# Quantised blocks: the second half of each normalisation moves from ScalarE to VectorE and GpSimd

## What is computed

```python
h = x
for blk in range(3):
    i0, i1 = (2 * blk, 2 * blk + 1)
    y = _qlora_linear(h, qweights[i0], scales[i0], biases[i0], lora_a[i0], lora_b[i0])
    y = _layernorm(y, ln_gamma[blk], ln_beta[blk])      # (y - mu) * rsqrt(var + 1e-5) * g + b
    y = jax.nn.gelu(y, approximate=False)
    y = _qlora_linear(y, qweights[i1], scales[i1], biases[i1], lora_a[i1], lora_b[i1])
    h = y + h
return h
```

## Time and profile before

| | |
|---|---|
| median of 3 runs | 1666.32 us |
| lowest and highest of them | 1662.14 and 1670.17 us |
| the profiled execution, own time | 1663.76 us |
| its span, first to last instruction | 1661.5 us |
| mean granted TensorE clock | 0.964 of full speed |
| busy share of the span: PE, DVE, ACT, POOL | 88%, 65%, 55%, 40% |

### The profile page before, as it was taken

The page is one execution under the profiler, slowest core; times in us unless marked ns, Lnnn a source line. Parts: engine busy times, 40 slices in busy tenths (PEclk is TensorE's granted clock), DMA queues, the critical chain, the costliest instruction groups (busy, mean ns, idle before and its releaser), DMA issues. The chain is left out here.

```text
span 1661.5 us, 30953 instructions
## 1 busy us (share of the span) xinstructions
PE 1470.2 (88%) x10541; PEld 1027.0 (62%) x10541; DVE 1079.1 (65%) x2724; ACT 920.5 (55%) x2444; POOL 658.3 (40%) x863
## 2 busy tenths in 40 slices
PE   7999999889989998999999895889889686999976
PEld 5667666666666665778787663555557533555643
DVE  5588888875666654555444346777523387899964
ACT  3578888555555563544544341334444258878945
POOL 5799999611111001003220253314534303888820
PEclk8999999999999997999999997999999887999999
DMA  9000000000000003000000114000012212333300
GB/s 296 14 1 14 14 15 15 13 1 1 1 1 1 1 1 119 1 2 21 18 17 21 44 60 173 2 1 13 30 54 61 75 35 47 90 85 87 91 12 25
DMA packets 48433, 65.36 MB, mean 39 GB/s; under 512 B 7839, under 2 KB 34568, under 8 KB 47530
## 3 DMA queue, kind: packets, MB, share of 16 engines
q1 hardware_dynamic: 43738, 54.02, 11.0%
q0 software_dynamic: 4544, 9.38, 1.6%
HBM read 52.80 MB, written 15.77 MB: 41 GB/s over the span
## 5 line engine op out<-in xcount | busy, mean ns | idle before, releaser
L2412 POOL TENSOR_TENSOR weighted<-state,c_all 128x512 f32<-128x512 f32 x128 | 163.5, 1297 | 78.7 <-DVE state L2422 64.8
L798 ACT ACTIVATE probs<-psum_all,pair_shift 128x256 f32<-128x256 f32 x256 | 117.8, 472 | 77.2 <-POOL pair_shift L487 77.2
L2422 DVE TENSOR_TENSOR_SCAN state<-decay,psum_all 128x512 f32<-128x512 f32 x128 | 149.0, 1200 | 14.3 <-PE psum_all L2340 11.5
L971 DVE TENSOR_REDUCE pair_negmax<-psum_all 128x2 f32<-128x512 f32 (+1 forms) x192 | 114.9, 639 | 55.9 <-PE psum_all L657 55.3
L2049 POOL DMA_INDIRECT found<-values,dest x78 | 74.7, 957 | 156.1 <-ACT values L2042 138.8
L798 ACT ACTIVATE probs<-psum_all,pair_negmax 128x192 f32<-128x192 f32 (+1 forms) x192 | 81.5, 436 | 93.6 <-DVE pair_negmax L971 46.3
L500 POOL TENSOR_SCALAR probs<-probs,pair_recip 128x256 f32<-128x256 f32 x128 | 121.8, 959 | 5.1 <-DVE pair_recip L991 5.1
L809 ACT ACTIVATE probsT<-psum_all 128x512 f32<-128x512 f32 x224 | 122.5, 612 | 0.3 <-PE psum_all L672 0.3
L2350 PE MATMUL psum_all<-weighted,ident 128*128 128x512 f32 x256 | 121.7, 600 | 0.0
L672 PE MATMUL psum_all<-ident,probs 128*128 128x128 f32 x896 | 116.7, 273 | 0.1
L487 POOL TENSOR_SCALAR pair_shift<-pair_negmax,row_term 128x1 f32<-128x1 f32 x256 | 102.2, 418 | 34.9 <-DVE pair_negmax L971 34.9
(11 more groups left out here) (402 smaller groups left out, 3510.5 us busy)
## 6 DMA issues: line engine op xcount, KB each, us to landing
c_all<-c_rows SPq DMA_DIRECT2D x64, 256.0 KB, 3.3
slots<-slot_fill_dram SPq DMA_DIRECT2D x2, 2535.0 KB, 14.4
ring<-slots SPq DMA_DIRECT2D x18, 260.0 KB, 2.9
keys<-found SPq DMA_DIRECT2D x16, 256.0 KB, 4.6
scale_rows<-row_scales SPq DMA_DIRECT2D x8, 256.0 KB, 4.6
up<-up_dram SPq DMA_DIRECT2D x1, 2048.0 KB, 7.8
down<-down_dram SPq DMA_DIRECT2D x1, 2048.0 KB, 13.0
up<-up_dram SPq DMA_DIRECT2D x1, 1408.0 KB, 6.1
```

The source lines that it names most:

```text
L798: nc.scalar.activation(k.probs[:, 2 * (u % PAIR_BUF) + j, t, key_cols(u, t)], k.psum[score_bank(u, j)][:, score_cols(u, t)], ACT.Exp, bias ...
L971: nc.vector.reduce_max(k.pair_negmax[:, u % 2, SUB * j:SUB * (j + 1)], src, AXX, negate=True).then_inc(s.negmax_ready, 1)
L2412: nc.gpsimd.tensor_tensor(w.weighted[:, u % RING, :], w.state[:, u % RING, :], w.c_all[:, u // L3_DC % C_RING, :], ALU.mult)\
L2422: nc.vector.tensor_tensor_scan(w.state[:, u % RING, :], w.decay[:, u % L3_RING, :, :].rearrange("p b n -> p (b n)"), k.psum[u % PARTS_RING ...
```

## The change

VectorE and GpSimd normalise the tiles of a block's second couple (chunks 2 and 3): GpSimd the first tile of each chunk (`BY_POOL` = 1), VectorE the other three. Each subtracts the mean and multiplies by rstd in one `tensor_scalar`, so the second couple needs no `scales`. ScalarE does root and both normalises for the first couple, then only the root for the second couple, then the GELUs. The one semaphore `normed` becomes three. TensorE's `keep_running` before second(0) goes from 4 products to 2, in every block, and in the first block 3 products into bank 7 are put before turn(0).

```diff
+        BY_POOL = 1
+        def by_act(u):
+            return u % CHUNKS < 2
+        def halves(u):
+            return 2 * (u // CHUNKS) + u % 2 + 1
+        def wait_normed(engine, u):
+            if by_act(u):
+                engine.wait_ge(s.act_normed, CT * halves(u))
+            else:
+                engine.wait_ge(s.pool_normed, BY_POOL * halves(u))
+                engine.wait_ge(s.dve_normed, (CT - BY_POOL) * halves(u))
+        def wait_couple_normed(engine, i):
+            wait_normed(engine, 2 * i + 1)
+        def normalise_tile(vector, t, signal):
+            vector.tensor_scalar(w.y[:, t, :], w.y[:, t, :], k.moments[:, t, 0:1], k.rstd[:, t:t + 1], ALU.subtract, ALU.mult).then_inc(signal, 1)
...
+            @block.gpsimd
+            def _(pool):
+                for blk in range(BLOCKS):
+                    pool.wait_ge(s.rstd_ready, 2 * blk + 2)
+                    for c in (2, 3):
+                        for t in range(CT * c, CT * c + BY_POOL):
+                            normalise_tile(nc.gpsimd, t, s.pool_normed)
...
                 def turn(u):
-                    pe.wait_ge(s.normed, CT * (u + 1))
+                    wait_normed(pe, u)
...
+                    if blk == 0:
+                        keep_running(nc, k, 7, 3)
                     turn(u)
                     turn(u + 1)
-                    keep_running(nc, k, u % CHUNKS, 4)
+                    keep_running(nc, k, u % CHUNKS, 2)
                     second(u)
...
                 def normalise(u):
-                    act.wait_ge(s.scales_ready, u // 2 + 1)
+                    act.wait_ge(s.scales_ready, u // CHUNKS + 1)
...
                 for blk in range(BLOCKS):
-                    for i in (2 * blk, 2 * blk + 1):
-                        root(i)
-                        normalise(2 * i)
-                        normalise(2 * i + 1)
+                    root(2 * blk)
+                    normalise(CHUNKS * blk)
+                    normalise(CHUNKS * blk + 1)
+                    root(2 * blk + 1)
                     for u in range(CHUNKS * blk, CHUNKS * (blk + 1)):
                         gelu(u)
...
                     if i >= 2:
-                        dve.wait_ge(s.normed, 2 * CT * (i - 1))
+                        wait_couple_normed(dve, i - 2)
...
+                def normalise(i):
+                    dve.wait_ge(s.rstd_ready, i + 1)
+                    for u in (2 * i, 2 * i + 1):
+                        for t in list(range(TILES))[chunk_tiles(u)][BY_POOL:]:
+                            normalise_tile(nc.vector, t, s.dve_normed)
...
                 moments(1)
-                scales(1)
+                normalise(1)
...
                     moments(2 * blk + 3)
-                    scales(2 * blk + 3)
+                    normalise(2 * blk + 3)
```

More of the change, by code:

```diff
@@ L2470, in quantised_ffn_stage @@
     UNITS = BLOCKS * CHUNKS
-    with signals(nc, "first_made", "biased", "dve_step", "moments_ready", "rstd_ready", "scales_ready", "normed", "turned", "gelu_ready", "second_made",
+    with signals(nc, "first_made", "biased", "dve_step", "moments_ready", "rstd_ready", "scales_ready", "act_normed", "dve_normed", "pool_normed", "turned", "gelu_ready", "second_made",
                  "h_ready", "h_turned", "x_added", "stored") as s:
@@ L2556, in normalise @@
                         nc.scalar.activation(w.y[:, t, :], w.y[:, t, :], ACT.Identity, scale=k.rstd[:, t:t + 1],
-                                             bias=w.shift[:, t:t + 1]).then_inc(s.normed, 1)
+                                             bias=w.shift[:, t:t + 1]).then_inc(s.act_normed, 1)
                 def gelu(u):
```

## The result

The changed kernel takes 1657.90 us in the median of 7 runs (1653.41 to 1659.88), the kernel before 1665.83 us in the 7 runs beside it (1662.14 to 1670.17). The ratio is 0.9954, 95% interval 0.9940 to 0.9968: 7.7 us faster by the ratio, with 5.3 to 10.0 inside the interval, and 7.9 us between the two medians. Forecast were 11.65 us off and 1654.7 us. The direction is right and the time lies in the range; the size is two thirds of the forecast.

What follows compares the result with a forecast made beforehand. Bound taken: a chain of hand-overs, with eight normalising tiles and a table load on ScalarE before the first GELU. 10.24 + 1.66 - 0.05 - 0.2 = 11.65 us off 1666.32 gives 1654.7 us; range 1649.5 to 1661.

Steps and rivals of the forecast that it cites:

- Part 1: ScalarE between second root and first GELU: shift and eight tiles leave the wait, GELU 1.53 us after root; 10.24 us gained.
- third rival: The GELU comes early, but VectorE or the next statistics set the block anyway: about 1664 to 1666 us; chance 0.08.
- fourth: Rival: halved filler loses the clock, TensorE at 1.2 GHz from second(0) to next root, about 1672 us; chance 0.04.
- Parts 2 and 3: Six tiles on VectorE, two on GpSimd, hidden before add_back(0) and turn(2) even under full exclusion: cost 0, bounds 0 to 1.5 us a block.
- second rival: VectorE and GpSimd exclusion costs more than its cover: 1.5 us a block, 4.6 in all, 1659.3 us; chance 0.08.
- Part 4: TensorE's filler before second(0), clock held at 2.4 GHz: 0.05 us lost in block one, 1.66 us gained in block three.
- first rival: Clock not held everywhere: 1.96 us lost in block one, 1.66 in block three; one 1656.5, both 1658.3 us; chance 0.27.
- Part 5: Semaphores: turn(2) and turn(3) wait for two signals, two more semaphores cleared; cost 0.2 us, bounds 0 and 0.5.
- R: The start of a block's second root on ScalarE; the GELU was forecast to start 1.53 us after it.

Runs made afterwards that it cites:

- experiment 7: The changed kernel with all eight tiles of the second couple on GpSimd, none on VectorE: ratio 0.9953 to the kernel before, stage 55.12 us.
- experiments 2: The changed kernel with the kernel before's filler (4 products before second(0), none before turn(0)): ratio 0.9951 to the kernel before, stage 54.58 us.
- `filler_turns`: The changed kernel plus one filler product between turn(0) and turn(1) of every block: ratios 0.9911 and 0.9942 to the kernel before, stage 51.16 and 51.14 us.

## Why the prediction was right, and where it was not

**Part 1, ScalarE, right.** 3.4 us a block: part 2 of the stage went from 19.29 to 15.87 or 15.86 in all three executions of the changed kernel. The GELU starts 1.52 us behind the second root in every block (1607.93 to 1609.45, 1625.21 to 1626.73, 1641.09 to 1642.61), forecast 1.53. With that the third rival is out (the gain is not absorbed) and so is the fourth: no part of the stage became longer.

**Parts 2 and 3, cost 0, right, for another reason.** I had let the two engines exclude each other and found that even so add_back(0) would be met. They do not. Complete exclusion would have ended the eight tiles 3.5 us behind the root; they end at 2.1 (second block). The single held instruction of the earlier trace rows was no guide to these tiles. The Trainium skill (SBUF — State Buffer, "Who interferes with whom") says that beside a VectorE instruction in a two-port mode the engine that comes second is blocked completely. The tiles here, one and the same tensor_scalar on both engines, lengthen by 14% and 7%, so for them the measurement decides, and it is against exclusion. In which mode VectorE ran them, no trace here shows. The second rival is out, and experiment 7 shows what it would have looked like: who is late is turn(3), by 1.1 us.

**Part 4, the clock, wrong, and this is the step that failed.** "I take the clock as held there" in block one, and the 1.66 us of block three as gained. In three executions of three the clock fell at turn(1) of the first block (in one of them 0.2 us before it) and before turn(1) of the third. The first block lost 1.40 us of its part, where the first rival had priced 1.96; the third lost 1.31, by the filler's end and a slow second(0), where the rival had 1.66. I had judged by the longest idle time alone, and those all became shorter. I had not looked at how little work lies between them: in the first block TensorE was busy for 0.72 us of the 3.0 before the fall. With one filler product between the turns the clock held in the first block in all four executions that had it, and in none of the ten without it. That is shown. By what rule the clock falls is not: the second and the third block look alike up to the third's turn(0), and one keeps the clock and the other does not. Why the third block lost it in three executions and kept it in experiments 2 and 7 stays open too.

**Part 5, too much.** The two-signal waits cost nothing that can be seen: part 2 has the 15.87 worked out without them, and `filler_turns` the 51.16 against 51.17.

**The sum.** 63.07 - 11.65 is 51.42; the changed kernel has 53.83, and 51.39, 51.16 and 51.14 were measured once the clock held in the first block. The forecast was that of a kernel with one more filler product a block. The first rival, both blocks lost, had 8.0 us off, 1658.3; measured are 7.9 off and 1657.9 in the medians. That is the case that came, and I gave it 0.27 against 0.53. The close match of the figure is partly luck: in the stage itself 9.24 us came off and not 8.0, since the low clock cost less than the rival had priced, and the interval of the whole time (5.3 to 10.0) holds both. The chance of more than 0.5% off, 0.76, was too high for the same reason: the measured 0.46% is just inside.

**Open:** the profiled stage is 9.2 to 9.4 us shorter and the whole time 7.7 to 8.8 us by three ratios. Whether the rest of the program gives back part of it can't be told from these. Over all eleven kernels here with the new order the stage is 9.8 us shorter on average and the whole time 9.4 (from the ratios), so that little is given back if anything; they share the runs of the kernel before, and in single ones stage and whole differ by some 3 us at most. Not tested is the nearest other edit: to leave the eight tiles on ScalarE, but behind the first two GELUs. At 0.40 us a tile chunk 2 would be ready some 4.6 us behind the root, an estimate from R + 1.53, two GELUs in 1.45 us and four tiles, where turn(2) wants it at 3.5.

## What to carry to other kernels

Work that stands on one engine between a root and an activation that does not need it is worth moving to idle engines, even where a tile takes twice as long there (GpSimd 0.8 us, ScalarE 0.40), because it then runs beside the table load and the GELU. When a filler product stands in front of a product on the path, work out its end at the low clock too, not only at the high one: the same four instructions took 1.9 or 3.0 to 3.4 us here, and only the first fits under the GELU. Put filler into the gaps ahead of the place where the clock is needed, in pieces no longer than the gap, and look in the trace whether it holds: here it did in the first block four times of four, and once it did not in the second. Judge an edit of filler only together with the order it stands in: the same one cost 2.8 us of stage under the old order and gained 0.75 under the new, both read from single executions.

## What the runs showed of the hardware

- VectorE and GpSimd tensor_scalar tiles of 128x128 fp32 on the same tile buffer ran side by side: 390 and 851 ns, against 342 and 798 where one engine had all of them.
- The load of an activation table took 1.28 us on ScalarE, and the GELU began 0.01 us behind it (1625.44 + 1.28 to 1626.73).
- The clock can fall without a long idle stretch: the longest one before the fall in the first block of the changed kernel was 1.4 us, where the kernel before kept it through 3.0 us in its second block. Its pattern of falls repeated in three executions on at least two chips, as did each part of the stage, to 0.12 us.
- The start of the stage, which no edit touched, lay between 1592.9 and 1600.4 us on one chip and between 1607.0 and 1609.9 on two others. A change of a few microseconds is to be read from its stage, not from the spans.
